# Row maxima turned in fp32 instead of three bf16 parts, with the feed-forward slices cut at whole pieces and the projections reordered

## The reference

```python
q, k, v = project(layernorm(x), Wq, bq), project(ctx, Wk, bk), project(ctx, Wv, bv)   # 16 heads x 8 x 4 "sup" channels
q, k, v = each + 0.1 * amp * einsum('bhsdi,hij->bhsdj', each, interference)
scores  = einsum('bhqdm,bhkdm->bhqkm', q, k) / sqrt(8)         # 64 softmaxes per sequence
x = x + (softmax(scores, over k) @ v) @ Wo.T + bo
gate, up = layernorm(x) @ dequant4bit(qweight_gu)              # 512 -> 2 * 1376
x = x + (silu(gate) * up) @ dequant4bit(qweight_down)          # 1376 -> 512
```

## Time and profile before

| what | us |
|---|---|
| median of 3 runs | 938.86 (938.69 to 940.8) |
| the profiled execution | 941.57 |
| its span, first to last instruction | 939.8 |
| TensorE busy in it | 757.6 |
| VectorE busy | 550.0 |
| ScalarE busy | 429.2 |
| GpSimd busy | 324.5 |

### The profile page before, as it was taken

The page is one execution under the profiler, slowest core; times in us unless marked ns, Lnnn a source line. Parts: engine busy times, 40 slices in busy tenths (PEclk is TensorE's granted clock), DMA queues, the critical chain, the costliest instruction groups (busy, mean ns, idle before and its releaser), DMA issues.

```text
span 939.8 us, 23081 instructions
## 1 busy us (share of the span) xinstructions
PE 757.6 (81%) x9441; PEld 530.1 (56%) x9441; DVE 550.0 (59%) x1141; ACT 429.2 (46%) x806; POOL 324.5 (35%) x290
## 2 busy tenths in 40 slices
PE   5405566666998899889988988898889989999798
PEld 5303322221577467746774777477647764776485
DVE  7987765655566456645764576357635763556421
ACT  1326466656355345534462446254526442654220
POOL 6643155425224412431243125212621352144211
PEclk9757655555899999999999999999999999999999
DMA  8900232121010020002000200020002000100000
GB/s 244 296 1 1 59 80 61 53 68 54 23 28 2 13 63 22 2 13 73 13 2 13 84 1 3 20 75 1 3 27 69 2 2 24 26 2 3 24 1 23
DMA packets 20702, 36.97 MB, mean 39 GB/s; under 512 B 3374, under 2 KB 7602, under 8 KB 20592
## 3 DMA queue, kind: packets, MB, share of 16 engines
q1 hardware_dynamic: 20604, 35.48, 13.0%
HBM read 26.56 MB, written 4.19 MB: 33 GB/s over the span
## 4 chain that ended last, share of the span: by engine, by line
issue 46%; PE 19%; POOL 14%; DVE 12%; ACT 6%; DMA 2%; SPq 1%; POOLq 0%; ACTq 0%; DVEq 0%
POOL arena L1357 8%; PE bank L513 4%; POOL arena L1344 3%; PE bank L528 3%; PE bank L494 2%; PE bank L484 2%; PE bank L445 2%; POOL arena L1335 2%; PE bank L448 2%; DMA arena<-in_L_xattn_Wo 2%; PE bank L446 2%; DVE arena L973 2%; DVE arena L1082 1%; ACT arena L776 1%; DVE nmf L1154 1%
## 5 line engine op out<-in xcount | busy, mean ns | idle before, releaser
L513 PE MATMUL bank<-arena,WGU 128*128 128x256 f16 (+1 forms) x2112 | 250.3, 275 | 8.5 <-DVE arena L1130 7.1
L513 PEld LDWEIGHTS bank<-arena,WGU 128*128 128x128 f16 (+1 forms) x2112 | 205.2, 101 | 36.7 <-DVE arena L1130 9.0
L1357 POOL TENSOR_TENSOR arena<-arena 128x512 f16<-128x512 f32 x128 | 145.0, 1161 | 207.8 <-ACT arena L855 207.8
L528 PE MATMUL bank<-WD,arena 128*128 128x512 f16 (+1 forms) x528 | 125.7, 387 | 9.3 <-DVE arena L1130 9.3
L484 PE MATMUL bank<-arena,WT 128*128 128x256 f16 x768 | 91.8, 280 | 40.4 <-DVE arena L708 39.2
L1344 POOL TENSOR_TENSOR arena<-arena 128x512 f16<-128x512 f32 (+1 forms) x48 | 51.6, 1075 | 207.9 <-ACT arena L828 207.9
L484 PEld LDWEIGHTS bank<-arena,WT 128*128 128x128 f16 x768 | 76.6, 100 | 56.0 <-issue 43.2
L848 ACT ACTIVATE arena<-bank,small 128x512 f32<-128x512 f32 x128 | 77.6, 688 | 36.9 <-PE bank L643 36.8
L494 PE MATMUL bank<-WT,arena 128*128 128x512 f16 x384 | 89.0, 387 | 1.8 <-DVE arena L706 1.8
L1154 DVE TENSOR_REDUCE nmf<-bank 128x8 f32<-128x512 f32 x128 | 81.5, 683 | 14.4 <-PE bank L617 14.4
L1106 DVE SCALAR_TENSOR_TENSOR arena<-arena,small 128x512 f16<-128x512 f32 x64 | 45.3, 749 | 70.8 <-ACT arena L812 70.8
(11 more groups left out here) (161 smaller groups left out, 1062.8 us busy)
## 6 DMA issues: line engine op xcount, KB each, us to landing
arena<-in_L_ffn_qweight_gu SPq DMA_DIRECT2D x8, 688.0 KB, 5.6
arena<-arena SPq DMA_DIRECT2D x32, 144.0 KB, 2.6
WT<-in_ctx SPq DMA_DIRECT2D x8, 512.0 KB, 15.2
arena<-in_ctx SPq DMA_DIRECT2D x8, 512.0 KB, 3.5
arena<-in_x SPq DMA_DIRECT2D x8, 512.0 KB, 3.6
out_y<-arena SPq DMA_DIRECT2D x16, 256.0 KB, 2.1
arena<-in_L_ffn_qweight_down SPq DMA_DIRECT2D x10, 256.0 KB, 3.4
arena<-in_L_xattn_Wk SPq DMA_DIRECT2D x1, 1024.0 KB, 5.9
```

The source lines that it names most:

```text
L513: mm = e.matmul(pb[0:m, i * TOK:(i + 1) * TOK], WGU[:, sp, kb, half * INTER + fb * P:half * INTER + fb * P + m], x2T[:, mp, kb, :], start= ...
L528: mm = e.matmul(pb[:, :], hT[0:m, sp, fb, t * P:(t + 1) * P], WD[0:m, mp, fb, :], start=(n == 0), stop=(n == 3 * FB - 1))
L1357: e.tensor_tensor(phl[:, a, 1, :], pring[:, a, :], phl[:, a, 0, :], ALU.subtract).then_inc(S["p_lo"], 1)
```

## The change

`sel` and `nmT` become fp32, and so does the turn of the maxima, which is now a transpose of `nmf` (the maxima in an array padded to 32 columns per head group). The four split operations go; LIFT goes into the bias of the exponential. `dve_max` is called four times in a row ahead of the slice. The slices get other sizes (`PRE, EACH, TAIL`). Steady chunks project keys, then transpose x2, then project queries, then slice 0, then values, then slice 1. In a batch the turn comes one slice earlier, and the turned scores come ahead of the slice that they followed. `act_p_hi` and `pool_p_lo` of steps 4b+2 and 4b+3 move to the start of the next batch. The transposes for the next chunk are spread otherwise.

```diff
-EXTRAS = (("cT0",), ("cT1",), ("xT0",), ("xT1", "oT0"))
+EXTRAS = ((("cT0",), ("cT1",)), ((), ()), (("xT0",), ("xT1",)), (("oT0",), ()))
...
-PRE, EACH, TAIL = (16, 26), (20, 22, 8, 24), (16, 16, 10, 16)
+PRE, EACH, TAIL = (24, 24), (24, 6, 18, 24), (12, 16, 14, 18)
...
-        nmf = sb("nmf", [P, 32], F32)
-        nrest = sb("nrest", [P, 32], F32)
-        nm16 = sb("nm16", [P, 4, 4, 8], BF16)
-        nmT = sb("nmT", [P, P], BF16)
-        sel = sb("sel", [P, KB, P], BF16)
+        nmf = sb("nmf", [P, 4, 32], F32)
+        nmT = sb("nmT", [P, P], F32)
+        sel = sb("sel", [P, KB, P], F32)
...
-            for t in range(TILES):
-                pe_rows(e, 2, t, AB[2 + t], cxT, S["proj_done"])
-                if not first and t == 0:
-                    e.wait_ge(S["y_ready"], 2 * c)
-                    for i in range(TILES):
-                        pe_transpose_tile(e, c, f"x2T{i}", xln, S["x2ln_ready"], 2 * (c - 1) + i + 1)
...
+            else:
+                e.wait_ge(S["y_ready"], 2 * c)
+                for i in range(TILES):
+                    pe_transpose_tile(e, c, f"x2T{i}", xln, S["x2ln_ready"], 2 * (c - 1) + i + 1)
             for G in range(2):
                 reached(e, S["x2_part"], 2 * c - 1 + G)
                 pe_project(e, 0, G, JB[G], xnT)
-                if not first and G == 0:
-                    e.wait_ge(S["t_lo"], t_at(c, "x2T1"))
-                ffn_slice(G)
+            if not first:
+                e.wait_ge(S["t_lo"], t_at(c, "x2T1"))
+            ffn_slice(0)
+            if not first:
+                for t in range(TILES):
+                    pe_rows(e, 2, t, AB[2 + t], cxT, S["proj_done"])
+            ffn_slice(1)
...
                 if b:
                     pe_values(e, c, 2 * b - 2)
+                pe_turn_max(e, c, b)
+                pe_extras(e, c, EXTRAS[b][0])
                 ffn_slice(slot[1])
+                pe_scores_turned(e, c, b)
                 if b:
                     pe_values(e, c, 2 * b - 1)
-                pe_turn_max(e, c, b)
-                pe_extras(e, c, b)
                 ffn_slice(slot[2])
-                pe_scores_turned(e, c, b)
+                pe_extras(e, c, EXTRAS[b][1])
                 ffn_slice(slot[3])
...
-            e.wait_ge(S["nm_split"], NB * c + b + 1)
-            e.matmul(AB[0][:, 0:P], nm16[:, :, :, :].rearrange("p a k n -> p (a k n)"), ident16[:, :],
-                     start=True, stop=True).then_inc(S["nm_turned"], 1)
+            e.wait_ge(S["max_done"], SLOTS * c + 4 * b + 4)
+            e.transpose(AB[0][:, 0:P], nmf[:, :, :].rearrange("p a n -> p (a n)"), ident[:, :]).then_inc(S["nm_turned"], 1)
...
-            e.activation(pring[:, a, :], AB[a][:, :], ACT.Exp, scale=KSM).then_inc(S["exp_done"], 1)
+            e.activation(pring[:, a, :], AB[a][:, :], ACT.Exp, bias=LIFT, scale=KSM).then_inc(S["exp_done"], 1)
...
+                if b:
+                    act_p_hi(e, c, 4 * b - 2)
+                    act_p_hi(e, c, 4 * b - 1)
                 act_slot(e, c, slot[0], first)
-                act_slot(e, c, slot[1], first)
                 act_copy_max(e, c, b)
...
-        def dve_split_max(e, c, b):
...
             dve_mask(e, c, 2, 0, 0)
+            if not first:
+                dve_v(e, c, 0, 5)
+            dve_mask(e, c, 3, 0, 1)
+            if not first:
+                dve_v(e, c, 1, 6)
             dve_slot(e, c, 0, first)
...
-                dve_max(e, c, 4 * b), dve_max(e, c, 4 * b + 1)
+                for a in range(4):
+                    dve_max(e, c, 4 * b + a)
                 dve_slot(e, c, slot[0], first)
-                dve_max(e, c, 4 * b + 2), dve_max(e, c, 4 * b + 3)
-                dve_split_max(e, c, b)
```

More of the change, by code:

```diff
@@ L462, in pe_transpose_tile, with pe_extras @@
             mm.then_inc(S["tr_done"], 1)
-        def pe_extras(e, c, b):
-            for name in EXTRAS[b]:
+        def pe_extras(e, c, names):
+            for name in names:
                 if name not in (T_LAST if is_last(c) else T_ORDER):
@@ L855, in act_p_hi, with act_v_hi @@
             e.activation(phl[:, a, 0, :], pring[:, a, :], ACT.Copy).then_inc(S["p_hi"], 1)
[L857 to L866, removed]
+        def act_v_hi(e, c):
             for t in range(TILES):
@@ L871, in act_chunk @@
                              pring[:, 2 + t, :].rearrange("p (h q n) -> p h q n", h=HEADS, q=2), ACT.Copy).then_inc(S["v_hi"], 1)
+        def act_chunk(e, c, first=False, last=False):
+            act_qk(e, c, 0, 1, 0)
             if first:
+                act_whi(e, 2)
+            else:
+                act_hi(e, c, "x2T0"), act_hi(e, c, "x2T1")
+            act_qk(e, c, 1, 1, 1)
+            if first:
+                act_whi(e, 3)
+                act_scale_part(e, 1)
+                act_v_hi(e, c)
                 e.wait_ge(S["wlo_done"], 3)
@@ L875, in act_chunk @@
                 act_scale_part(e, 2)
-            act_qk(e, c, 4, 0, 0)
+            act_qk(e, c, 4 if first else 2, 0, 0)
+            act_qk(e, c, 5 if first else 3, 0, 1)
             act_slot(e, c, 0, first)
-            act_qk(e, c, 5, 0, 1)
+            if not first:
+                act_v_hi(e, c)
             act_slot(e, c, 1, first)
@@ L892, in act_chunk @@
                 act_exp(e, c, 4 * b + 3)
+                act_slot(e, c, slot[2], first)
                 act_p_hi(e, c, 4 * b)
                 act_p_hi(e, c, 4 * b + 1)
+                for name in EXTRAS[b][1]:
+                    if name in (T_LAST if last else T_ORDER):
+                        act_hi(e, c, name)
                 act_slot(e, c, slot[3], first)
-                act_p_hi(e, c, 4 * b + 2)
-                act_p_hi(e, c, 4 * b + 3)
+            act_p_hi(e, c, SLOTS - 2)
+            act_p_hi(e, c, SLOTS - 1)
             for k in AT_TAIL[:3]:
@@ L1182, in dve_apply_next, with dve_v, dve_v_lo @@
                 ln_apply(e, "x", c + 1, t, xin[:, t, :], S["xln_ready"])
+        def dve_v(e, c, t, turn):
+            e.wait_ge(S["proj_done"], 6 * c + turn)
+            reached(e, S["p_lo"], SLOTS * c - 1 + t)
+            e.scalar_tensor_tensor(pring[:, 2 + t, :], AB[2 + t][:, :], KV, bv_row[:, :], ALU.mult, ALU.add).then_inc(S["v_evicted"], 1)
+        def dve_v_lo(e, c):
+            for t in range(TILES):
+                e.wait_ge(S["v_hi"], 2 * c + t + 1)
+                e.tensor_tensor(ap(vsb[:, t], 0, P, 18, [(VROW, HEADS), (HEADS * VROW, 2), (1, 16)]),
+                                pring[:, 2 + t, :].rearrange("p (h q n) -> p h q n", h=HEADS, q=2),
+                                ap(vsb[:, t], 0, P, 0, [(VROW, HEADS), (HEADS * VROW, 2), (1, 16)]), ALU.subtract).then_inc(S["v_lo"], 1)
         def dve_chunk(e, c, first=False, last=False):
@@ L1190, in dve_chunk @@
                 dve_wlo(e, 2)
+            else:
+                dve_lo(e, c, "x2T0"), dve_lo(e, c, "x2T1")
             dve_mask(e, c, 1, 1, 1)
@@ L1193, in dve_chunk @@
                 dve_wlo(e, 3)
[L1194 to L1205, removed]
+                dve_v(e, c, 0, 3), dve_v(e, c, 1, 4)
+                dve_v_lo(e, c)
                 dve_lo(e, -1, "xT0"), dve_lo(e, -1, "xT1")
@@ L1208, in dve_chunk @@
             dve_mask(e, c, 2, 0, 0)
+            if not first:
+                dve_v(e, c, 0, 5)
+            dve_mask(e, c, 3, 0, 1)
+            if not first:
+                dve_v(e, c, 1, 6)
             dve_slot(e, c, 0, first)
-            dve_mask(e, c, 3, 0, 1)
+            if not first:
+                dve_v_lo(e, c)
             dve_slot(e, c, 1, first)
@@ L1213, in dve_chunk @@
                 slot = IN_BATCH[b]
-                dve_max(e, c, 4 * b), dve_max(e, c, 4 * b + 1)
+                for a in range(4):
+                    dve_max(e, c, 4 * b + a)
                 dve_slot(e, c, slot[0], first)
-                dve_max(e, c, 4 * b + 2), dve_max(e, c, 4 * b + 3)
-                dve_split_max(e, c, b)
                 if b:
                     dve_o(e, c, 2 * b - 2)
+                for name in EXTRAS[b][0]:
+                    if name in (T_LAST if last else T_ORDER):
+                        dve_lo(e, c, name)
                 dve_slot(e, c, slot[1], first)
@@ L1222, in dve_chunk @@
                     dve_o(e, c, 2 * b - 1)
-                for name in EXTRAS[b]:
+                dve_slot(e, c, slot[2], first)
+                for name in EXTRAS[b][1]:
                     if name in (T_LAST if last else T_ORDER):
                         dve_lo(e, c, name)
-                dve_slot(e, c, slot[2], first)
                 if b == 0 and not last:
```

36 lines of the change are left out of this document (14 added, 22 removed).

## The result

The changed kernel takes **906.35 us** (median of 4 runs, 906.22 to 906.91) where the one before took 938.78 beside it: ratio 0.9654, 95% interval 0.9636 to 0.9671. That is 3.5% faster.

What follows compares the result with a forecast made beforehand. TensorE was taken to bound the seven steady chunks. Waits -46, turn +1.7, fp32 `sel` +50 and chunk 0 +10 gave +16 us on 938.86, so 955 us, with a range from 907 to 986.

Steps and rivals of the forecast that it cites:

- the staircase: Turned scores: a low half waiting for its group holds back the next group's high; +0.45 us a quarter, 50 us lost.
- side by side: Turned scores, bound from below: all four row groups run at once, +0.17 us a quarter, 0.67 a batch; chance 0.27.
- serial: Turned scores, bound from above: no fp32 matmuls overlap, +0.83 us a quarter, 3.3 a batch; 1009 us, chance 0.18.
- the first rival: Turned scores: groups truly side by side, 0.67 us a batch added, 914 us in all; chance 0.27.
- the two cases: Turned scores: the staircase, 1.8 us a batch, or groups side by side, 0.67 us a batch.
- Waits, split and turn: Steady-chunk waits gain 46 us, chunk 0's removed split gives -4, the fp32 turn adds 1.7.
- the walk: TensorE followed through a new steady chunk: 2.1 us of waits left, 15 in all of 60.6, so 46 us gained.
- the thin margin: Steady chunk's start: x2 transposes directly after keys keep 1.1 us of cover behind the norm's last apply, so no wait.

Runs made afterwards that it cites:

- one bf16 part: The changed kernel with `sel` and `nmT` in bf16 instead of fp32, the turn itself still fp32: 873.88 us, ratio 0.9305.
- group by group: The changed kernel with each head group's three fp16 and one fp32 matmuls of a quarter in a row, instead of rounds over the groups: 912.08 us, ratio 0.9711.
- the filler: The kernel before with six unused 512-column matmuls put into TensorE's 1.5 us wait ahead of the first attention-output transpose: 937.22 us, ratio 0.9969.
- The old head: The changed kernel with the old order of keys, values, x2 transposes and queries at a steady chunk's start, on all engines: 923.02 us, ratio 0.9829.
- the old sizes: The changed kernel with the slice sizes (`PRE, EACH, TAIL`) of the kernel before: 949.92 us, ratio 1.011.
- the maxima two and two: The changed kernel, new slices, with two maxima ahead of the first slice's multiply and two behind it: 964.97 us, ratio 1.0286; with old slices 962.13.
- the roundings: The changed kernel with the moved `act_p_hi` and `pool_p_lo` back at the end of their batch: 906.87 us, ratio 0.9656.
- the norm early: Next chunk's layer-norm statistics (VectorE) and rstd (GpSimd) moved earlier in the changed kernel: 896.78 us; with old slice sizes 909.89; with bf16 `sel` and `nmT` 865.55.

## Why the prediction was wrong

The miss is 955 - 906.35 = 48.7 us and has two parts: what fp32 costs, from the changed kernel against the one with one bf16 part, and the rest, from that one against the kernel before.

**fp32 `sel`: forecast 50 + 14.5, measured 32.5 (32 of the miss).** The step that failed is "the staircase": "Low 0 waits for its own group until 0.11; high 1 may start only then." The trace has four halves together and the other four 0.17 later, and in "group by group" fp16 matmuls of other groups start between a group's two halves, so a waiting low half doesn't hold back the next group. The added time of a quarter is 0.44 - 0.23 = 0.21, against 0.45 (staircase), 0.17 (side by side) and 0.83 (serial). Over a batch it is 0.88 (1.89 us for the turned scores against 1.01), 25 us in 28 batches, against 50 forecast. The mechanism is that of the first rival; its size was near too, 0.67 a batch. The argument that the order of the bf16 rounds never asks a matmul to overtake was right, and it should have left the two cases even instead of deciding between them. The Trainium skill's rule in TensorE: Matmul & The Clock Gate, Part 3, that matmuls start and end in program order, is contradicted here by the single fp32 instructions between fp16 ones in "group by group". The Trainium skill's TensorEngine Tiling (Array Packing), Key Properties, says that different tiles can load and multiply in parallel, and that is what the trace shows.

In chunk 0 the forecast was 3.6 a batch at half clock, 14.5 in all. The two kernels differ by 6.9 there, which is what 0.88 a batch gives at half clock (4 x 2 x 0.88 = 7.0). Chunk 0 as a whole grew by 4.0, not 10.

**Waits, split and turn: forecast -46 - 4 + 1.7 = -48, measured -65 (17 of the miss).** Most of the named waits went as the walk said: none for the masks, none for the x2 transposes despite the thin margin, none for the multiplies or `oT0`. The turn waits 1.09 in batch 1, where 1.5 was forecast, 0.44 in batch 2, where none was, and not at all in batch 0, where 0.3 to 0.4 was: 1.5 a chunk where 2.1 was left. From 60.6 to 9.2 + 1.3 they fell by 50.1 in the steady chunks, within the bounds of 30 to 58. What was mis-sized is the price of a wait, taken as its idle time alone. Each has a tail besides. The timeline of TensorE of the kernel before has slice 1 ahead of the first scores of the earlier trace rows:

```profile
447.87 3.00 PE L513 MATMUL bank<-arena,WGU 128*128 128x256 f16 x26
```

From there to the scores at 452.57 are 4.70 us, and 26 x 0.109 + 1.70 = 4.53: the wait costs 0.17 more than its idle time, and there are 58 waits before against 17 after. The clock dips behind some of the longer ones too: chunks with a dip last 92.5 to 92.9 us, full ones without 91.4 and 91.6; the filler, which ended the dips, gained 3 us net of its own cost. By an estimate from these figures the tails are 41 x 0.17 = 7 us and the dips 4 x 1.2 = 5; the other 5 of the 17 stay open.

**The turn** steps by 0.17 (446.60 to 446.77), not 0.11, some 1.7 us more than forecast in 28. **The exponential's bias** was put at nothing. One takes 776 ns where it took 688, 88 ns more each; the Trainium skill's ScalarE: Activation LUTs, What ACT_TABLE_LOAD costs, gives about 93 ns for each operand read per partition. No wait of TensorE shows it.

**Where the gain of the order lies.** The old head costs 16.7 us, the old sizes 43.6, the maxima two and two 58.6 (964.97 against 906.35), the roundings nothing. The earlier place of the turn and of the turned scores was not tested by itself. The prediction walked the slices and found no wait, but never asked what the old sizes would do in the new order, and so didn't see that whole pieces are what covers the late layer norm. These effects aren't additive: with the norm early, the old sizes cost 13.1.

## What to carry to other kernels

Where independent row groups each issue a pair of dependent matmuls, measure a small case before choosing between the bounds; here four pairs ran side by side, 0.27 us for all eight halves, and cost 32.5 us where 64.5 were forecast. When TensorE waits for another engine, look at what stands ahead of the releaser in that engine's list: two steps of the next chunk's norm (statistics and rstd), moved to an earlier place, gave back 40 us in one kernel and 10 in another, and 8 in the one with one bf16 part. Count a wait at more than its idle time, since a tail follows it and behind some of the long ones here a slower clock, and ask whether a value that only shifts a softmax needs fp32 at all, since that alone was worth 32 us.

## What the runs showed of the hardware

Four 32-row fp32 matmuls, eight instructions, start as two bursts of four, 0.17 us apart, with the next fp16 round 0.10 behind. With the matmuls issued group by group, three fp16 instructions start between two single fp32 ones (449.68 and 449.75), so order of start is not the program's order across row groups. The granted clock fell to 0.57 to 0.59 for some 4 us, so for most of them it was at the lower of its two levels, 1.2 of 2.4 GHz, after stretches of 3 to 4 us in which TensorE was busy for 0.80 of 3.40 or 2.33 of 4. It didn't fall behind every such stretch: three of the seven steady chunks of the kernel before kept 1.00. In the changed kernel, whose longest wait in a steady chunk is 1.1 us, it never fell there.
